# The first half's state sums by accumulating transposes, without pair additions, and a new order of the work

## The chip, the cores and the metric

The kernel runs on one core of a Trainium2 chip, in one launch. The metric is device time in microseconds from the first to the last instruction of the execution; the change is judged by the median of several executions. Engines are named as the profile names them: PE (TensorE), DVE (VectorE), ACT (ScalarE), POOL (GpSimd) and SP (SyncE, which only issues DMAs here).

## What is computed

Eight batches of 512 tokens with 128 features go through two layers, each of the form `x = x + s(xn) * silu(f(xn))` with `xn = layernorm(x)`. The first has attention and a mixture of 8 experts (top 2) side by side. The second has a Mamba block and 8 experts of which each token takes the best one:

```python
def _selective_scan(u, delta, A, Bm, Cm, D):
    def step(s, inp):
        d_t, B_t, C_t, u_t = inp
        s = s * exp(d_t[..., None] * A) + d_t[..., None] * B_t[:, None, :] * u_t[..., None]
        return (s, einsum('bds,bs->bd', s, C_t))
    ...
    return ys.swapaxes(0, 1) + u * D

scores = feats @ centroids.T
expert = argmax(scores, axis=1)
alpha = sigmoid(sum(feats * centroids[expert], axis=-1, keepdims=True))
```

The Mamba block has 256 inner channels (`d`, two halves of 128) and 16 states per channel; its input goes through an RMS norm first, `h = xn * rsqrt(mean(xn * xn) + eps)`. Each expert norms its input again.

## The kernel before

**Layout.** A tile is 128 partitions by 512. For the scan the partitions are inner channels and the columns are the 512 tokens of a batch, so half `h` (0 or 1) of the channels and state `n` (0 to 15) make scan step `s = 2n + h`, 32 steps per batch. For each step ACT computes the decay `dA` (step `d`), PE spreads row `n` of B over the partitions (`b`, into `b_row`), DVE multiplies it with `du` and runs the scan (L1328, L1341), POOL multiplies the state with row `n` of C (`p`, L1518). The products are summed over `n`: those of half 0 on PE into the PSUM bank `yacc`, by a matmul with the identity (`a`, L919), after a first product with `diagD` that adds `u * D` (L912); those of half 1 on POOL into `y1` (`e`, L1525), in the last batch on PE too (L927). The states live in few slots of `st` (three for half 0, two for half 1), so a scan waits until its slot's last user has been summed.

**Pair additions.** With `PAIRED = (4, 8, 12)`, DVE adds the products of states `n - 1` and `n` of half 0 (`q`, `add_pair`, L1347) and PE sums the result once, so 13 sums stand for 16 states.

**After the sums.** Step `y` (`c_step`, L1353 to L1360) gates both halves on DVE and writes them into `du`, reading `yacc` and reusing it for half 1; `op` projects them back (L936), and POOL or DVE adds the residual.

**Second experts.** ACT norms the tokens (`xm`) to `xn1_tok`, and scales them by `rstd2` to `ht_tok`, which shares memory with `rl`. PE transposes both (`hT`, L791; `x1T`, L787), ACT copies both out of PSUM. `sc` multiplies x1T with the centroids, DVE takes the maximum `am` and the choice (`first_max`), `rk` finds each token's place, and `put` scatters the rows of `xn1_tok` by an indirect DMA of POOL. The experts' work is group `F` (`w` loads of weights, `xs`, `h`, `y`), and `get` gathers their rows, `ft` and `silu` finish them.

**Order.** Nothing is planned while it runs. The table `ROWS` gives each step of each group a place in units of a batch (group A: attention and first experts, two batches ahead; H: norm to delta, one ahead; S: the scan; F: second experts; C: output of the batch before), a lag for ACT, DVE and POOL in 32nds of a batch, and a PSUM bank out of four. `OWN` gives the first two batches' A and H their own places, `P` rows prepare weights. `program(engine)` sorts all steps by place and lag; each engine works its own list strictly in that order and waits on semaphores where data come from another. `READY`, `EMPTY` and `BEFORE` count what each semaphore must have reached. So a step that waits holds all that stands behind it on its engine.

Of the kernel before, what the change touches and what calls it, by code (L numbers as in the profile page):

```python
# [28 lines left out]
E = 8  # L29
# [13 lines left out]
PAIRED = (4, 8, 12)  # L43
# [10 lines left out]
def adds_of_first(n):  # L54

    m, k = n % NS, n // NS
    return k * (NS - len(PAIRED)) + m + 1 - sum(1 for p in PAIRED if p <= m)


def group_tiles(k):  # L60
# [1544 lines left out]
```

## Time and profile before

| | |
|---|---|
| time, median of 3 runs | 950.92 us (949.97 to 953.21) |
| span of the profiled execution | 950.8 us, 15737 instructions |
| first scan starts | 133.4 us |
| scans of batch 7 start | 867.3 us |
| last DVE instruction starts | 947.5 us |
| mean granted PE clock | 0.951 |

```profile
DVE  3352678999889998999989998899899999998994
PEclk9997999999899989999999999999899998886998
L1341 DVE TENSOR_TENSOR_SCAN st<-dA,b_row 128x512 f32<-128x512 f32 x123 | 148.8, 1210 | 8.0 <-ACT dA L975 7.8
L1347 DVE TENSOR_TENSOR st<-st 128x512 f32<-128x512 f32 x24 | 28.2, 1175 | 0.9
L919 PE MATMUL yacc<-st,w_ident 128*128 128x512 f32 x208 | 115.7, 641 | 21.9 <-POOL st L1518 16.5 <-DVE st L1347 5.3
```

The first two lines cut the span into 40 equal slices and give the share in which DVE was busy, and the clock that PE was granted, in tenths. The others are groups of instructions of one form: how many, their busy time in us and the mean of one in ns, then how long the engine had been idle before them and which instruction ended that. An fp32 matmul of 512 columns leaves two records. PE is pipelined: a record is longer than the distance to the next.

### The profile page before, as it was taken

What the parts mean: (1) busy time and instruction counts of PE and PEld (TensorE: products, weight loads), DVE (VectorE), ACT (ScalarE), POOL (GpSimd) and SP (SyncE); (2) the same over time, 40 slices, a digit from 0 to 9 for tenths busy, and PEclk for the clock granted to TensorE, in tenths of its full rate; (3) what the DMA queues carried; (4) which work ended last, traced back from release to release, by engine and by line L of the source; (5) the groups of instructions that cost most, each with busy time, mean ns of one, the idle gap of its engine ahead of it and who ended that gap; (6) DMA issues with size and microseconds to landing.
All of it is one profiled execution on the core that took longest, in us unless ns stands there. A gap on an engine that the chain in (4) does not pass through costs nothing.

```text
span 950.8 us, 15737 instructions
## 1 busy us (share of the span) xinstructions
PE 831.6 (87%) x4576; PEld 575.2 (61%) x4576; DVE 798.4 (84%) x1503; ACT 629.8 (66%) x1379; POOL 604.9 (64%) x556
## 2 busy tenths in 40 slices
PE   4989999998899879998799869998899876866885
PEld 2767666764677547765576547765676644543552
DVE  3352678999889998999989998899899999998994
ACT  2534667777687856776687866776686865684561
POOL 0000125769585884769585885769585888788664
PEclk9997999999899989999999999999899998886998
DMA  7200122232332333232331333232331333343441
GB/s 261 101 1 1 47 73 85 75 114 78 119 98 77 110 108 82 77 109 80 118 103 68 103 118 84 81 103 86 108 108 62 106 113 107 105 110 103 149 128 38
DMA packets 79430, 90.29 MB, mean 95 GB/s; under 512 B 8450, under 2 KB 49906, under 8 KB 78834
## 3 DMA queue, kind: packets, MB, share of 16 engines
q1 hardware_dynamic: 77298, 85.07, 29.4%
q0 software_dynamic: 2048, 4.20, 1.5%
q8 instruction: 40, 0.66, 0.3%
q14 instruction: 44, 0.36, 0.1%
HBM read 52.96 MB, written 13.04 MB: 69 GB/s over the span
## 4 chain that ended last, share of the span: by engine, by line
PE 39%; DVE 38%; issue 11%; POOL 6%; ACT 5%; SPq 1%; DVEq 0%; DMA 0%; POOLq 0%; ACTq 0%
DVE st L1341 13%; PE work L849 7%; PE work L855 6%; DVE acc L1225 4%; DVE b_row L1328 3%; PE work L890 3%; PE work L880 3%; PE work L778 3%; DVE cv L1254 3%; DVE dbu L1328 3%; POOL st L1518 2%; PE yacc L919 2%; DVE st L1347 2%; ACT prob L975 1%; PE work L769 1%
## 5 line engine op out<-in xcount | busy, mean ns | idle before, releaser
L1518 POOL TENSOR_TENSOR st<-st,Cs 128x512 f32<-128x512 f32 x249 | 320.0, 1297 | 158.0 <-DVE st L1341 152.8
L975 ACT ACTIVATE dA<-delta,Aneg 128x512 f32<-128x512 f32 x256 | 177.7, 718 | 12.9 <-DVE st L1341 12.8
L1341 DVE TENSOR_TENSOR_SCAN st<-dA,b_row 128x512 f32<-128x512 f32 x123 | 148.8, 1210 | 8.0 <-ACT dA L975 7.8
L1341 DVE TENSOR_TENSOR_SCAN st<-dA,dbu 128x512 f32<-128x512 f32 x128 | 154.6, 1208 | 0.0
L1525 POOL TENSOR_TENSOR y<-y,st 128x512 f32<-128x512 f32 x105 | 138.1, 1315 | 3.8
L849 PE MATMUL work<-xnT,w_w1a 128*128 128x512 f32 x256 | 132.7, 612 | 8.5 <-DVE delta L1309 7.0
L855 PEld LDWEIGHTS work<-w_w2a,hid 128*128 128x128 f32 x1024 | 125.1, 196 | 23.4 <-issue 8.7
L919 PE MATMUL yacc<-st,w_ident 128*128 128x512 f32 x208 | 115.7, 641 | 21.9 <-POOL st L1518 16.5
L975 ACT ACTIVATE hsT<-work,hs 128x128 f32<-128x128 f32 x352 | 100.2, 370 | 46.5 <-PE work L880 45.9
L855 PE MATMUL work<-w_w2a,hid 128*128 128x128 f32 x1024 | 128.8, 280 | 0.7 <-ACT hid L975 0.6
L880 PEld LDWEIGHTS work<-xsT,hs 128*128 128x128 f32 x704 | 98.6, 207 | 25.1 <-issue 5.9
L975 ACT ACTIVATE hid<-work,w_b1a 128x512 f32<-128x512 f32 x128 | 86.2, 683 | 37.6 <-PE work L849 33.3
L880 PE MATMUL work<-xsT,hs 128*128 128x128 f32 x704 | 103.2, 294 | 2.6 <-ACT ys L975 1.4
L1225 DVE SCALAR_TENSOR_TENSOR acc<-work,gates,acc 128x128 f32<-128x128 f32 x256 | 71.3, 340 | 35.2 <-PE work L855 32.8
L890 PE MATMUL work<-w_w2f,hsT 128*128 x704 | 99.2, 284 | 0.0
L1328 DVE TENSOR_TENSOR dbu<-b_row,du 128x512 f32<-128x512 f32 x123 | 85.1, 692 | 13.2 <-PE b_row L903 5.9
L890 PEld LDWEIGHTS work<-w_w2f,hsT 128*128 128x128 f32 x704 | 86.0, 192 | 5.7 <-issue 3.0
L1328 DVE TENSOR_TENSOR b_row<-b_row,du 128x512 f32<-128x512 f32 x123 | 84.0, 683 | 2.7
L849 PEld LDWEIGHTS work<-xnT,w_w1a 128*128 128x128 f32 x256 | 43.4, 192 | 42.3 <-issue 17.1
L919 PEld LDWEIGHTS yacc<-st,w_ident 128*128 128x128 f32 x208 | 37.0, 202 | 52.7 <-POOL st L1518 25.4
L1488 POOL DMA_INDIRECT xs_dram<-xn_tok,pos x32 | 32.2, 1006 | 57.6 <-DVE pos L1303 51.2
L903 PE MATMUL b_row<-bc,sel_b 96*128 96x512 bf16 x123 | 48.5, 394 | 21.9 <-DVE st L1341 21.9
(191 smaller groups left out, 1290.9 us busy)
## 6 DMA issues: line engine op xcount, KB each, us to landing
Cs<-c_dram SPq DMA_DIRECT2D x128, 256.0 KB, 3.6
hs<-w_w1f SPq DMA_DIRECT2D x88, 258.0 KB, 2.3
xs_in<-xs_dram SPq DMA_DIRECT2D x16, 256.0 KB, 3.4
ys_dram<-ys SPq DMA_DIRECT2D x16, 256.0 KB, 2.9
w_w1f<-in_w1f_dram SPq DMA_DIRECT2D x1, 2064.0 KB, 8.0
x_in<-in_x_dram SPq DMA_DIRECT2D x8, 256.0 KB, 5.6
w_w2f<-in_w2f_dram SPq DMA_DIRECT2D x1, 2048.0 KB, 12.4
kept_dram<-x_tok SPq DMA_DIRECT2D x8, 256.0 KB, 4.0
```

The source lines that it names most:

```text
L849: last = mm(w[:], W["w1a"][:, i * 128:(i + 1) * 128], xnT[:], start=True, stop=True)
L855: last = mm(w[:, t * 128:(t + 1) * 128], hid[:, c % 4, t * 128:(t + 1) * 128], W["w2a"][:, c * 128:(c + 1) * 128], start=(c == PER * i), s ...
L880: last = mm(w[:, c * 128:(c + 1) * 128], w1s[:, i % 2, c * 128:(c + 1) * 128], xsT[:, i // 4 % 2, i % 4 * 128:(i % 4 + 1) * 128], start=Tr ...
L890: last = mm(r, hsT[:, i % 2, c * 128:(c + 1) * 128], W["w2f"][:, bass.ds(e * H1 + c * 128, 128)], start=False, stop=(c == HC - 1))
L903: mm(rows_bank(n, b)[:], row_of(n), bc3[:, par], start=True, stop=True).then_inc(sig["B_in"], 1)
L919: mm(yacc[:], ident[:], state(s), start=False, stop=(n == NS - 1)).then_inc(sig["y_sum0"], 1)
L975: return nc.scalar.activation(out, in_, func, **k)
L1225: last = V.scalar_tensor_tensor(acc[:, t], w[:, t * 128:(t + 1) * 128], gates[:, t, i:i + 1], acc[:, t], ALU.mult, ALU.add)
L1328: V.tensor_tensor((dbu0, rows_bank(n, b))[h][:], rows_bank(n, b)[:], du[:, par, h], ALU.mult).then_inc(sig["dBu"], 1)
L1341: V.tensor_tensor_scan(state(s), dA[:, s % DECAYS], (dbu0, rows_bank(n, b))[h][:], 0.0, ALU.mult, ALU.add).then_inc(sig["scan"], 1)
L1518: G.tensor_tensor(state(s), state(s), Cs[:, b.of(NS, n) % C_BUFS], ALU.mult).then_inc(sig["P"], 1)
L1525: G.tensor_tensor(y1[:], y1[:], state(s), ALU.add).then_inc(sig["y_sum1"], 1)
```

## The change

- The steps `q` and `PAIRED` are gone: every product of half 0 is summed by itself. The wait of a scan for its slot is now always for the sum.
- In batches 0 to 6 a sum of half 0 is four transposes of 128x128 with the state as stationary operand and the identity as moving one, accumulated into `yacc`, which then holds the sum with tokens on the partitions. After the last one ACT copies `yacc` into `delta[:, par, 0]` (new step `yt`), and PE forms `u * D` in a bank of `work` and adds four transposes of the copy to it (new step `yb`). DVE's `y` reads that bank. `yacc` is free once `yt` has read it.
- In batch 7 the sums stay identity matmuls, now 16, and `y` reads `yacc`.
- `x1T`, its transposes and its copy are gone. `sc` multiplies hT, which is scaled by `rstd2`, and DVE multiplies the maximum with `rms` (POOL: `q2 * rstd2`), the inverse of that scale.
- `ht_tok` has its own memory; `put` scatters its rows in place of those of `xn1_tok`, so `xm` waits for the `put` of the batch before. ACT's `dl` of half 1 waits for `sc`, since `rl` shares memory with hT.
- All places, lags of moved steps, own places and banks are new. On DVE, `y` of a batch now stands behind scans 0, 1 and 2 of the next batch and two sums of first experts (m6, m7), where it stood behind scan 0. On POOL, `ft` moved behind the first product of the next batch, and the four `get` stand among the last products of a batch.

```diff
-PAIRED = (4, 8, 12)
...
-    ("H", "x1T", 0, 0.46354, -1, 7, -3, 1),
-    ("S", "q", 4, 0.32753, 3, 1, 6, None),
-    ("S", "q", 8, 0.61830, 4, 0, 2, None),
-    ("S", "q", 12, 0.85132, -1, 0, 2, None),
...
+    ("C", "yt", 0, 0.15021, -5, 0, 0, None),
+    ("C", "yb", 0, 0.04512, 0, 0, 0, 0),
...
             def add_state(n, b):
 
                 s = NH * n
+                last = b.is_(NB - 1)
                 if n == 0:
                     if b.is_(0):
                         pe.wait_ge(prep_dve, 3)
-                    since(pe, sig["yo"], b.of(1))
-                    mm(yacc[:], diagD[:], u[:, b.n % 2, 0], start=True, stop=False)
-                if n + 1 in PAIRED:
+                    since(pe, sig["yt"], b.of(1))
+                    if last:
+                        mm(yacc[:], diagD[:], u[:, b.n % 2, 0], start=True, stop=False)
+                pe.wait_ge(sig["P"], b.of(STEPS, s + 1))
+                if last:
+                    mm(yacc[:], ident[:], state(s), start=False, stop=(n == NS - 1)).then_inc(sig["y_sum0"], 1)
                     return
-                if n in PAIRED:
-                    pe.wait_ge(sig["pair"], b.of(len(PAIRED), PAIRED.index(n) + 1))
-                else:
-                    pe.wait_ge(sig["P"], b.of(STEPS, s + 1))
-                mm(yacc[:], ident[:], state(s), start=False, stop=(n == NS - 1)).then_inc(sig["y_sum0"], 1)
+                for t in range(NT):
+                    add = mm(yacc[:, t * 128:(t + 1) * 128], state(s)[:, t * 128:(t + 1) * 128], ident[:], is_transpose=True,
+                             start=(n == 0 and t == 0), stop=(n == NS - 1), skip_group_check=True)
+                add.then_inc(sig["y_sum0"], 1)
+
+            def turn_back(g, step, b):
+
+                par = b.n % 2
+                w = bank(g, step, b)
+                bank_free(pe, g, step, b)
+                pe.wait_ge(sig["yt"], b.of(1, 1))
+                mm(w[:], diagD[:], u[:, par, 0], start=True, stop=False, skip_group_check=True)
+                for t in range(NT):
+                    part = slice(t * 128, (t + 1) * 128)
+                    last = mm(w[:, part], delta[:, par, 0, part], ident[:], is_transpose=True, start=False, stop=True,
+                              skip_group_check=True)
+                last.then_inc(ready[g], 1)
...
+                    since(act, sig["put"], b.of(16 * NT))
...
+                elif g == "C" and name == "yt" and not b.is_(NB - 1):
+                    act.wait_ge(sig["y_sum0"], b.of(NS, NS))
+                    go(delta[:, b.n % 2, 0], yacc[:], ACT.Copy).then_inc(sig["yt"], 1)
...
+                    dve.wait_ge(sig["rms"], b.of(1, 1))
+                    V.tensor_tensor(am[:], am[:], rms[:], ALU.mult)
...
-            def add_pair(n, b):
-
-                dve.wait_ge(sig["P"], b.of(STEPS, NH * n + 1))
-                V.tensor_tensor(state(NH * n), state(NH * n), state(NH * (n - 1)), ALU.add).then_inc(sig["pair"], 1)
...
+                    if not last:
+                        dve.wait_ge(sig["yo"], b.of(1, 1))
+                        dve.sem_inc(free_of("C", ("yb", 0), b), 1)
```

## Rows read from the trace of the kernel before

**Rows 1.** The page, busy time and chain that ended last.
```profile
PE 831.6 (87%) x4576; PEld 575.2 (61%) x4576; DVE 798.4 (84%) x1503; ACT 629.8 (66%) x1379; POOL 604.9 (64%) x556
...
PE 39%; DVE 38%; issue 11%; POOL 6%; ACT 5%; SPq 1%; DVEq 0%; DMA 0%; POOLq 0%; ACTq 0%
```

**Rows 2.** Windows: stretch, busy us (x) of each engine, PEclk, DMA share, GB/s.
```profile
455.00:561.00 106.00, 95.43 (x560) 66.95 (x560) 98.00 (x185) 78.25 (x172) 78.22 (x72) 1.00 0.31 97
...
775.00:867.00 92.00, 64.32 (x299) 41.63 (x299) 86.10 (x122) 56.07 (x126) 73.54 (x67) 0.82 0.37 106
867.00:951.00 84.00, 64.84 (x309) 40.46 (x307) 66.08 (x79) 39.65 (x99) 54.24 (x43) 0.93 0.37 112
```

**Rows 3.** Timeline of DVE, start and length in us.
```profile
242.55 0.69 DVE L1353 TENSOR_TENSOR du<-yacc,zg 128x512 f32<-128x512 f32 x1
...
778.45 0.69 DVE L1353 TENSOR_TENSOR du<-yacc,zg 128x512 f32<-128x512 f32 x1
```

**Rows 4.** Waits of DVE from 247 to 785 us: total, times, longest.
```profile
DVE gm L1196 <- PE work L748: 6.2, 5, 2.2
...
DVE nmax L1192 <- PE work L763: 1.8, 5, 0.4
```

**Rows 5.** Timeline of DVE, first and third pair addition of a steady batch.
```profile
492.51 0.92 DVE L1347 TENSOR_TENSOR st<-st 128x512 f32<-128x512 f32 x1
493.35 1.11 DVE L1225 SCALAR_TENSOR_TENSOR acc<-work,gates,acc 128x128 f32<-128x128 f32 x4
...
543.58 1.42 DVE L1347 TENSOR_TENSOR st<-st 128x512 f32<-128x512 f32 x1
544.91 0.69 DVE L1307 SCALAR_TENSOR_TENSOR work<-work,ez 128x512 f32<-128x512 f32 x1
```

**Rows 6.** Timeline of DVE, pair additions of batches 6 and 7.
```profile
851.34 4.00 DVE L1347 TENSOR_TENSOR st<-st 128x512 f32<-128x512 f32 x1
855.27 0.69 DVE L1307 SCALAR_TENSOR_TENSOR work<-work,ez 128x512 f32<-128x512 f32 x1
...
926.79 0.67 DVE L1347 TENSOR_TENSOR st<-st 128x512 f32<-128x512 f32 x1
927.37 0.69 DVE L1328 TENSOR_TENSOR work<-work,du 128x512 f32<-128x512 f32 x1
```

**Rows 7.** Timeline of DVE, a small operation behind a drain.
```profile
468.84 0.19 DVE L1204 SCALAR_TENSOR_TENSOR eq<-gt,w_first 128x32 f32<-128x32 f32 x1 [0.21 <-DVE ot L1368]
```

**Rows 8.** Timeline of PE, a sum and four transposes in a full queue.
```profile
462.41 0.60 PE L744 MATMUL work<-w_ident,qkv 128*128 128x128 f32 x4
462.85 0.22 PE L888 MATMUL work<-b2p,sel_b 96*128 96x128 bf16 x1
...
501.82 1.02 PE L919 MATMUL yacc<-st,w_ident 128*128 128x512 f32 x2
502.68 0.38 PE L903 MATMUL b_row<-bc,sel_b 96*128 96x512 bf16 x1
```

**Rows 9.** Groups of instructions by form: count, busy us, mean ns, idle before.
```profile
L787 PE MATMUL work<-w_ident,xn_tok 128*128 128x128 f32 x32 | 4.8, 272 | 0.0
...
L975 ACT ACTIVATE xn1T<-work 128x512 f32<-128x512 f32 x8 | 4.7, 589 | 0.0
...
L1505 POOL DMA_INDIRECT fe<-ys_dram,pos x32 | 31.1, 972 | 7.5 <-issue 6.6
```

**Rows 10.** Timeline of DVE between batches 6 and 7.
```profile
870.47 0.69 DVE L1353 TENSOR_TENSOR du<-yacc,zg 128x512 f32<-128x512 f32 x1 [1.95 <-PE yacc L919]
...
873.30 0.76 DVE L1357 SCALAR_TENSOR_TENSOR yacc<-u,w_dskip,y 128x512 f32<-128x512 f32 x1 [2.14 <-POOL y L1525]
```

**Rows 11.** Timelines of PE and POOL at the end of a batch.
```profile
558.60 1.12 PE L919 MATMUL yacc<-st,w_ident 128*128 128x512 f32 x2 [0.88 <-POOL st L1518]
...
554.82 4.95 POOL L1518 TENSOR_TENSOR st<-st,Cs 128x512 f32<-128x512 f32 x4
```

More of the change, by code:

```diff
@@ L403, with turned_not @@
 TAKEN_AT = {("A", ("o", 0)): ("o", NT - 1)}
+def turned_not(step, b):
+    return step == ("C", ("yb", 0)) and b == NB - 1
 READY = {}
@@ L408 @@
 for _g, _s, _b in ORDER:
-    if (_g, _s) in BANK:
+    if (_g, _s) in BANK and not turned_not((_g, _s), _b):
         READY[_g, _s, _b] = 1 + sum(1 for g, s, b in READY if g == _g)
     _job = _g, TAKEN_AT.get((_g, _s), _s), _b
-    if _job[:2] in BANK and _job not in EMPTY:
+    if _job[:2] in BANK and _job not in EMPTY and not turned_not(_job[:2], _b):
         _k = bank_of(*_job)
@@ L495, in build @@
         hx = sb("hx", [128, NH, T])
-        ht_tok, hT = hx[:, 0].rearrange("p (i d) -> p i d", i=NT), hx[:, 1]
+        hT = hx[:, 1]
         rl = hx
@@ L515, in build @@
         rstd2 = sb("rstd2", [128, NT])
+        rms = sb("rms", [128, NT])
         shift, shift1 = sb("shift", [128, NT]), sb("shift1", [128, NT])
@@ L518, in build @@
         xn1_tok = sb("xn1_tok", [128, 2, NT, D])
-        xn1T = sb("xn1T", [128, T])
+        ht_tok = sb("ht_tok", [128, NT, D])
         u = sb("u", [128, 2, NH, T])
@@ L783, in a_step @@
                         last = nc.tensor.transpose(w[0:E, t * 128:(t + 1) * 128], gates[:, t], ident[:])
-                elif name == "x1T":
-                    pe.wait_ge(sig["xn1"], b.of(1, 1))
-                    for t in range(NT):
-                        last = nc.tensor.transpose(w[:, t * 128:(t + 1) * 128], xn1_tok[:, par, t], ident[:])
                 elif name == "hT":
@@ L800, in a_step @@
                 elif name == "sc":
-                    emptied(pe, g, ("x1T", 0), b)
+                    emptied(pe, g, ("hT", 0), b)
                     if b.is_(0):
@@ L953, in do @@
                     project(g, step, b)
+                elif g == "C" and name == "yb" and not b.is_(NB - 1):
+                    turn_back(g, step, b)
                 elif g == "P" and name == "pe":
@@ L1024, in a_step @@
                     go(tiles(bank(g, ("m", E - 1), b)[:]), acc[:], ACT.Tanh).then_inc(sig["siluA_e"], 1)
-                elif name == "x1T":
-                    filled(act, g, step, b)
-                    go(xn1T[:], w[:], ACT.Copy).then_inc(fr, 1)
                 elif name == "hT":
@@ L1351, in c_step @@
                 if step[0] == "y":
-                    dve.wait_ge(sig["y_sum0"], adds_of_first(b.of(NS, NS - 1)))
-                    V.tensor_tensor(du[:, par, 0], yacc[:], zg[:, par, 0], ALU.mult).then_inc(sig["y0"], 1)
+                    last = b.is_(NB - 1)
+                    if last:
+                        dve.wait_ge(sig["y_sum0"], b.of(NS, NS))
+                        r = yacc
+                    else:
+                        filled(dve, "C", ("yb", 0), b)
+                        r = bank("C", ("yb", 0), b)
+                    V.tensor_tensor(du[:, par, 0], r[:], zg[:, par, 0], ALU.mult).then_inc(sig["y0"], 1)
                     dve.wait_ge(sig["y_sum1"], b.of(NS, NS))
                     dve.wait_ge(sig["y0"], b.of(1, 1))
-                    second = work[SPARE] if b.is_(NB - 1) else y1
-                    V.scalar_tensor_tensor(yacc[:], u[:, par, 1], W["dskip"][:, 1:2], second[:], ALU.mult, ALU.add
+                    second = work[SPARE] if last else y1
+                    V.scalar_tensor_tensor(r[:], u[:, par, 1], W["dskip"][:, 1:2], second[:], ALU.mult, ALU.add
                                            ).then_inc(sig["y1"], 1)
                     dve.wait_ge(sig["y1"], b.of(1, 1))
-                    V.tensor_tensor(du[:, par, 1], yacc[:], zg[:, par, 1], ALU.mult).then_inc(sig["yo"], 1)
+                    V.tensor_tensor(du[:, par, 1], r[:], zg[:, par, 1], ALU.mult).then_inc(sig["yo"], 1)
+                    if not last:
+                        dve.wait_ge(sig["yo"], b.of(1, 1))
+                        dve.sem_inc(free_of("C", ("yb", 0), b), 1)
                 elif step[0] == "op":
@@ L1386, in do @@
                     scan(i, b)
-                elif g == "S" and name == "q":
-                    add_pair(i, b)
                 elif g == "C":
@@ L1476, in a_step @@
                         G.tensor_tensor(rstd2[:], q2[:], neghalf[:], ALU.pow).then_inc(sig["rstd1"], 1)
+                        pool.wait_ge(sig["rstd1"], b.of(1, 1))
+                        since(pool, sig["hot"], b.of(1))
+                        G.tensor_tensor(rms[:], q2[:], rstd2[:], ALU.mult).then_inc(sig["rms"], 1)
                 elif name == "du":
@@ L1489, in a_step @@
                                          bass.IndirectOffsetOnAxis(pos[:, par, i:i + 1], 0),
-                                         xn1_tok[:, par, i], None).then_inc(sig["put"], 16)
+                                         ht_tok[:, i], None).then_inc(sig["put"], 16)
             def f_step(step, b):
```

19 lines of the change are left out of this document (8 added, 11 removed), and 548 rows, old and new, of tables (OWN, OWN_BANKS, ROWS, sig).

## The prediction

> **What bounds the kernel now.** I read the busy times first [rows 1]: TensorE 87%, VectorE 84%, ScalarE and GpSimd two thirds, and the chain that ended last is split between TensorE and VectorE. An average of that kind names no bound, so the windows by period came next [rows 2]. In steady state a batch takes 107.2 us: the first product of a batch's output (L1353) starts at 242.6 us and, five batches on, at 778.5 us [rows 3]. In such a stretch of 106 us VectorE's records cover 98 us and TensorE's 95.4 us. In the last two stretches, where no later batch's attention is left, TensorE falls to 64 us of 92 and VectorE stays near 94% of the first of them.
>
> What VectorE's remaining 8 us are decides. Part of them are drains of about 0.2 us between dependent small operations. What it waits for others in five steady periods is 26.2 us in seven rows of the waits, 6.2 down to 1.8 us [rows 4], 5.2 us per period; five of the seven, 3.7 us per period, name TensorE as the releaser. So VectorE runs without a hole apart from 5 us: whatever is taken off its queue comes off the period, if TensorE follows. TensorE has about 10 us of holes per period, so it isn't the first bound but a close second.
>
> **Pair additions (VectorE).** The three `q` steps per batch go. Their price is the distance from their start to the next instruction's, since records overlap: 0.84, 0.90 and 1.33 us in one steady period (the first and the last of the three in [rows 5]), 3.07 us. For batches 0 to 5: 6 x 3.07 = 18.4 us. In batch 6 the third held the engine 3.93 us, in batch 7 each took 0.58 us [rows 6]: 0.84 + 0.90 + 3.93 = 5.7 us and 1.8 us. The spread has a reason: the add reads two SBUF tensors, and the dear ones stand beside a train of GpSimd products. The GPSIMD Engine Reference of the Trainium skill (Specifications) says that GpSimd shares its SBUF interfaces with VectorE where the latter has two SBUF inputs; the trace agrees, 0.58 us where GpSimd pauses and 3.93 us beside its train. What stands next in VectorE's queue there mostly reads PSUM, so I count the whole of it as gone. Sum: 25.9 us.
>
> **Additions to VectorE.** One 128x4 multiplication by `rms` per batch and, in seven batches, a wait for its own last product before the bank is given back. Neither is in the trace; the nearest row is a small operation of 0.19 us behind a drain of 0.21 us [rows 7]. Bounds 0.1 and 0.4 us for each, taken 0.2: 15 x 0.2 = 3.0 us lost.
>
> **The sums (TensorE).** A sum by identity matmul takes 0.86 us start to start in a full queue; four 128x128 fp32 transposes take 0.44 us [rows 8]. Before, 13 sums: 11.2 us per batch; after, 16 sums in seven batches: 7.0 us. The turn back adds four transposes (0.44), the x1T transposes go (0.44), the diagD product only moves. Saved: 4.1 us per period. The other bound: the state is now the stationary operand, so its load can't start ahead of the product as the identity's could, and four transposes alone last 0.60 us by the length of their record [rows 8]. Then 17 x 0.16 = 2.7 us are given back and 1.5 us remain. I take the full queue's value, since most sums stand behind other matmuls. None of it is on the path by itself; it buys cover for the waits of [rows 4]. In batch 7 the sums stay identity matmuls, 16 in place of 13, 2.6 us on an engine with 20 us of holes: nothing.
>
> **ScalarE** loses the copy of x1T and gains the copy of `yt`, 0.59 us each [rows 9]. GpSimd gains one 128x4 product per batch. `put` now sends rows of the single ht_tok, so `xm` of the next batch waits for it; in the new queues some 20 scans lie between them. Nothing for each. The last batch's `dl` wait for `sc` is met long before.
>
> **The end of a batch.** The output's path grows: last sum, ScalarE copy, TensorE turn back, then VectorE's `y`. Sorting the rows by place and lag gives the new queues: VectorE reaches `y` after scan 2 of the next batch, the products m6 and m7, and `silu`; before it stood behind scan 0 and `silu`. So the path has some 6 us more cover (two scans with their inputs 3.6, m6 and m7 2.4) for 1.9 us more work (copy 0.59, turn back 0.86 + 0.44). Where this matters is between batches 6 and 7: today VectorE stands 1.95 us for the sums and 2.14 us for the GpSimd half [rows 10]. Two more scans stand ahead of it now, and GpSimd's `ft` goes behind; of 4.1 us I take 3, bounds 0 and 4.1.
>
> **The new places.** They can't be priced by rows. The score maximum `gl`, the dearest of the waits [rows 4], stands three operations later, and TensorE has 4 us more room; of 5.2 us per period I take 1 in six periods, 6 us; bounds from 1 us worse to 3.7 us better (all that TensorE causes). In the last batch GpSimd issues its gathers between the last products instead of before them: four issues of about 1.25 us with their gaps [rows 9] now partly behind the last scan, about 1 us lost. The stages before the first scan (133 us) lose 0.44 us of TensorE work and are laid anew: nothing, within 3 us.
>
> **Sum.** 25.9 - 3.0 + 3 + 6 - 1 = 30.9 us. The profiled execution spans 950.8 us, 0.1 us under the median of 950.92 (949.97 to 953.21): 920.
>
> **Rivals.** (a) A wait takes the freed time. TensorE saves only 1.5 us, the waits stay (minus 6), the 3 us between batches stay, and the new order costs 1 us per period (7): 936. For it: TensorE is busy 95 of 106 us, and the holes of a new order can't be read from this trace. Against: it needs both at once. 18%.
> (b) The order does better: 3.7 of 5.2 us go in six periods, 16 more: 904. 11%.
> (c) TensorE's clock. In batch 6, where its queue thins, the granted clock is 0.82 against 1.00 [rows 2]. The new sums thin it too. TensorE's 91.3 us per period at 0.82 are 111.3 us, so it would bind, 4.1 us over today's period: +25 for six periods, less the 10.5 us of batches 6 and 7: 965, slower. It decides from a clock of 91.3 / 103 = 0.89 down. TensorE's page of the Trainium skill (TensorE: Matmul & The Clock Gate, Part 4) says that PE-mode transposes don't count as busy for the clock in the way matmuls do; by that rule this rival is the likely one where sums fill a thin stretch. This trace doesn't show it: the transposes it has (16 of prob per batch among them) lie in a period granted 1.00 [rows 2]. Against: transposes would be 7.4 us of 91. 3%.
> (d) A transpose with a fresh stationary state takes its own 272 ns [rows 9], not 110: 17 x 4 x 0.16 = 11 us more, TensorE 102 us plus its 10 us of holes: a period of 113, +34 less 10.5: 974, slower. 2%.
> (e) ScalarE blocks at `yt`: its queue holds the tanh and the next decays behind a wait for the last sum. Today four products run as a train, and the last sum starts 1.2 us before that train ends [rows 11]. In the new queues, counted from the end of delta, GpSimd has two du products, P29, a gather and P30 ahead of the last sum (6 us), sum and copy end at 7; VectorE has scans 29, 30, 31, 0, m6, m7, 1 and 2 ahead of the `silu` that needs the tanh (13 us). So 6 us of cover; each us beyond costs 7 us in all, and it is slower from 11 us on; at 12 us 962. 2%.
> (f) The additions weren't what held the scans, and all of their time comes back as waits for the same sums: 950.8 less the 3 us between batches, 948, no change. 2%. The main case: 62%.
>
> **Chances.** Faster by over 0.3% (2.9 us; about what a measurement of this kernel can tell from no change): 0.92, within: 0.02, slower: 0.06. Range 907 to 937: it takes in (a) and leaves half of (b) and all of (c) to (f) out, some 15 in 100, the rest being for bounds not met.
>
> **What would show it.** No L1347 rows; steady periods of 103 to 104 us; VectorE's covered time per period near 95 us with 4 us of waits; TensorE's near 91 us, the four-transpose sum 0.44 us start to start, the clock at 0.95 or more; no wait above 1 us at L1353 before the last batch. A TensorE-bound period (its holes under 5 us while VectorE's grow), or VectorE waiting for the bank of `yb`, would make the prediction wrong.

## The result and the profile after

The changed kernel takes 945.51 us, median of 9 runs (943.44 to 947.6), the one before 953.7 us in the same session (949.97 to 957.45): ratio 0.9913, 95% interval 0.9894 to 0.9932. Of the 30.9 us that were forecast, 8 came. The profiled execution spans 943.7 us. From its page, the busy times and the engines of the chain that ended last, which answer [rows 1]:

```profile
PE 815.7 (86%) x4844; PEld 607.9 (64%) x4844; DVE 799.8 (85%) x1487; ACT 630.5 (67%) x1378; POOL 597.8 (63%) x564
...
PE 42%; DVE 36%; issue 12%; ACT 5%; POOL 3%; DMA 1%; SPq 1%; DVEq 0%; POOLq 0%; ACTq 0%
```

TensorE's records cover 16 us less, VectorE's cover as much as before, although 24 additions of 128x512 are gone. Two facts stand in these lines already: something on VectorE grew, and TensorE, with less to do, leads the chain more than before.

**Where the time went.** The first scan of each batch cuts the execution (starts of the first of its 32 scans in VectorE's timeline; batch 7 ends with its last scan):

| stretch, us | before | after | forecast |
|---|---|---|---|
| start to first scan | 133.4 | 123.4 | same within 3 |
| batches 0 to 5 | 641.5 | 648.5 | 22 less |
| batch 6 | 92.4 | 90.3 | |
| batch 7 to its last scan | 65.4 | 63.8 | with batch 6 some 10 less |

So the loss is mainly in the steady batches, 7 us slower instead of 22 faster, and the stages before them gave 10 us that the forecast had put at nothing. Without these 10 us the changed kernel would not have been faster at all. The windows of batches 0 to 5, before and after (stretch, busy us of each engine, PEclk, DMA share, GB/s):

```profile
133.00:775.00 642.00, 587.13 (x3366) 412.46 (x3364) 586.42 (x1100) 469.82 (x1036) 463.09 (x421) 0.97 0.32 95
```
```profile
123.00:772.00 649.00, 577.54 (x3576) 437.42 (x3574) 588.64 (x1077) 470.36 (x1031) 453.84 (x422) 0.94 0.31 94
```

The granted clock fell from 0.97 to 0.94. Summed over windows of 1 us, 34 us of this part were at 1.2 GHz before and 71.5 us after; all numbers "at 1.2 GHz" below are such sums.

**VectorE's ledger, batches 0 to 5** (from each start to the next, waits apart): pair additions 18.1 to 0; waits for `b_row` 4.8 to 18.6; four small operations with two SBUF inputs 19 us more in sum; all idle times above 0.15 us together 38.6 to 43.4. The waits of VectorE after (total, times, longest), where [rows 4] had `gm` and `nmax`:

```profile
DVE dbu L1346 <- PE b_row L898: 18.6, 18, 2.3
DVE acc L1241 <- PE work L850: 8.4, 17, 1.1
```

**The first new cost: TensorE's clock.** TensorE's timeline at the end of batch 3 (start, length; in brackets the idle time before and its releaser), and the same stretch in windows:

```profile
541.61 0.39 PE L898 MATMUL b_row<-bc,sel_b 96*128 96x512 bf16 x1 [1.56 <-DVE st L1357]
541.84 1.02 PE L844 MATMUL work<-xnT,w_w1a 128*128 128x512 f32 x2
545.37 1.34 PE L844 MATMUL work<-xnT,w_w1a 128*128 128x512 f32 x2 [2.50 <-DVE delta L1327]
...
550.96 2.91 PE L850 MATMUL work<-w_w2a,hid 128*128 128x128 f32 x16
553.71 0.38 PE L898 MATMUL b_row<-bc,sel_b 96*128 96x512 bf16 x1
```
```profile
541.00:545.30 4.30, 1.25 (x3) 0.40 (x3) 4.23 (x7) 3.58 (x6) 3.27 (x4) 1.00 0.65 212
...
546.00:549.00 3.00, 2.22 (x9) 1.51 (x8) 2.97 (x4) 1.28 (x3) 2.77 (x6) 0.52 0.07 22
549.00:553.00 4.00, 4.00 (x15) 2.97 (x14) 2.92 (x4) 2.65 (x5) 3.84 (x4) 0.50 0.40 133
```

TensorE works 1.25 of 4.3 us, waiting for the last broadcast and for `delta`; then the clock stands at 0.5 for 7 us, of which it works 6.2. The 16 products of 128x128 take 2.91 us instead of 2.0, the next batch's first row of b goes out at 553.71, and VectorE stands for it:

```profile
554.18 0.70 DVE L1346 TENSOR_TENSOR dbu<-b_row,du 128x512 f32<-128x512 f32 x1 [2.26 <-PE b_row L898]
```

The sums themselves cost what the prediction had: in a full queue at the full clock the four transposes take 0.44 us from start to start (median of 69), a matmul with the identity 0.86 (51 of them before).

```profile
517.12 0.60 PE L915 MATMUL yacc<-w_ident,st 128*128 128x128 f32 x4
517.56 1.02 PE L844 MATMUL work<-xnT,w_w1a 128*128 128x512 f32 x2
```

**The second: small operations beside GpSimd.** VectorE and GpSimd of the changed kernel at the second gate:

```profile
513.38 0.19 DVE L1186 TENSOR_TENSOR eq<-work,am 128x32 f32<-128x32 f32 x1
513.60 1.21 DVE L1187 TENSOR_TENSOR eq<-eq,w_first 128x32 f32<-128x32 f32 x1
514.85 0.19 DVE L1188 TENSOR_REDUCE gr<-eq 128x4 f32<-128x32 f32 x1
515.07 0.97 DVE L1189 TENSOR_TENSOR ohr<-eq,gr 128x32 f32<-128x32 f32 x1
```
```profile
513.50 1.26 POOL L1539 TENSOR_TENSOR st<-st,Cs 128x512 f32<-128x512 f32 x1
514.73 1.26 POOL L1546 TENSOR_TENSOR y<-y,st 128x512 f32<-128x512 f32 x1
```

L1187 begins 0.1 us behind a GpSimd product and ends with it (514.81 and 514.76), L1189 behind the next and ends with that (516.04 and 515.99). The reduction between them has one input, L1186 reads one of its two from PSUM: neither is touched. (The 256 scans aren't either, 1.21 us beside GpSimd or not: one of their inputs, `b_row` or `dbu`, lies in PSUM.) Before, L1187's counterpart took 0.19 us at this place. The pattern repeats in every batch, and again at the first gate (1.18 and 0.97 us).

### The profile page after: what moved, and what is told of

Its sections match the earlier page's. It is cut to its first block, busy times and chain, and to the rows that moved or that the text cites. A ratio compares the mean times of both kernels' runs of the same rounds, so it can differ in the third digit from the quotient of the medians.

```text
span 943.7 us, 16309 instructions
## 1 busy us (share of the span) xinstructions
PE 815.7 (86%) x4844; PEld 607.9 (64%) x4844; DVE 799.8 (85%) x1487; ACT 630.5 (67%) x1378; POOL 597.8 (63%) x564
## 4 chain that ended last, share of the span: by engine, by line
PE 42%; DVE 36%; issue 12%; ACT 5%; POOL 3%; DMA 1%; SPq 1%; DVEq 0%; POOLq 0%; ACTq 0%
DVE st L1357 10%; PE work L850 9%; PE work L844 9%; DVE b_row L1346 4%; PE work L777 3%; DVE cv L1270 3%; DVE acc L1241 3%; PE work L875 3%; DVE dbu L1346 2%; PE work L885 2%; PE work L761 2%; PE yacc L915 2%; PE work L768 2%; POOL st L1539 1%; PE yacc L977 1%
## 5 line engine op out<-in xcount | busy, mean ns | idle before, releaser
L844 PE MATMUL work<-xnT,w_w1a 128*128 128x512 f32 x256 | 137.2, 626 | 16.8 <-DVE delta L1327 15.0
L850 PEld LDWEIGHTS work<-w_w2a,hid 128*128 128x128 f32 x1024 | 131.3, 205 | 18.2 <-issue 15.0
L850 PE MATMUL work<-w_w2a,hid 128*128 128x128 f32 x1024 | 134.2, 288 | 3.5 <-ACT hid L988 3.5
L1546 POOL TENSOR_TENSOR y<-y,st 128x512 f32<-128x512 f32 x105 | 133.5, 1271 | 5.2
L885 PE MATMUL work<-w_w2f,hsT 128*128 x704 | 102.5, 290 | 0.0
L885 PEld LDWEIGHTS work<-w_w2f,hsT 128*128 128x128 f32 x704 | 88.3, 197 | 3.2 <-issue 1.2
L915 PE MATMUL yacc<-w_ident,st 128*128 128x128 f32 x448 | 72.6, 291 | 3.6 <-POOL st L1539 3.6
L915 PEld LDWEIGHTS yacc<-w_ident,st 128*128 128x128 f32 x448 | 59.2, 155 | 20.4 <-issue 15.2
L1509 POOL DMA_INDIRECT xs_dram<-ht_tok,pos x32 | 32.2, 1006 | 61.8 <-DVE pos L1321 55.5
```

Of the source, the lines that this page charges most:

```text
L844: last = mm(w[:], W["w1a"][:, i * 128:(i + 1) * 128], xnT[:], start=True, stop=True)
L850: last = mm(w[:, t * 128:(t + 1) * 128], hid[:, c % 4, t * 128:(t + 1) * 128], W["w2a"][:, c * 128:(c + 1) * 128], start=(c == PER * i), s ...
L885: last = mm(r, hsT[:, i % 2, c * 128:(c + 1) * 128], W["w2f"][:, bass.ds(e * H1 + c * 128, 128)], start=False, stop=(c == HC - 1))
L915: add = mm(yacc[:, t * 128:(t + 1) * 128], state(s)[:, t * 128:(t + 1) * 128], ident[:], is_transpose=True, start=(n == 0 and t == 0), sto ...
L1546: G.tensor_tensor(y1[:], y1[:], state(s), ALU.add).then_inc(sig["y_sum1"], 1)
```

## The experiments

Two theories stood at first. *Places*: the mechanics give what was forecast, and the new places lose it. *Mechanics*: what VectorE is spared comes back wherever the places are. All times below are medians; ratios are to the kernel before, run beside them, with their 95% intervals.

**The mechanics on the old places, the pair additions alone, identity sums on the new places, b's first row earlier.**

> All mechanics of the change (no pair additions, sums by accumulating transposes, the copies yt and yb, scores without the rows of their own) on the places of before; only the additions of m 3 and m 7 are put a little earlier, and yt and yb stand just ahead of their readers. Places theory (the mechanics are worth what was forecast, and the new places lost it in the periods, through waits for b_row, 13.8 us more in batches 0 to 5, and through some 20 us of small VectorE operations that stand beside GpSimd's; their prologue gave 10 us back): the periods fall from 107.2 to 103 or 104 us, the time before the first scan stays at 133 us, and the whole is about 925 us (918 to 933). Mechanics theory (what VectorE is spared comes back wherever the places are, since the additions and drains only exchange one contention for another and TensorE sets the rest): the periods stay at 107 to 109 us and the whole is 945 to 957 us.

```diff
-PAIRED = (4, 8, 12)
+("C", "yt", 0, 0.00800, 0, 0, 0, None)
+("C", "yb", 0, 0.03150, 0, 0, 0, 0)
...
```

999.7 us, 1.0468 (1.0404 to 1.0532): batches 0 to 5 took 675 us. Neither theory had that. TensorE waits for x^T because `yb` keeps its bank (waits of PE there; L1366 is the give back of that bank):

```profile
PE work L729 <- DVEq L1366: 14.0, 5, 2.8
```

> The kernel before with the pair additions taken away and nothing else: TensorE sums all 16 states of the first half by matmuls with the identity, 3 more per batch (about 2.6 us of it per batch at 0.86 us each). If the freed VectorE time (3.07 us per period, 25.9 us in all by the profile of before) is really gone, the whole falls by 15 to 25 us, to 929 to 939 us. If the pair additions' time was contention that the next VectorE operations inherit (they took 0.6 us each when GpSimd rested), no more than 3 x 0.6 us per period and some 3 us at batches 6 and 7 go: 12 us at most, less what TensorE has to do more: 941 to 953 us.

```diff
-PAIRED = (4, 8, 12)
+PAIRED = ()
...
-    ("S", "q", 4, 0.32753, 3, 1, 6, None),
```

The edit also moves the sums of states 3 and 7, which the pairs had made needless, to earlier places, 0.352 and 0.567. 956.5 us, 1.0029 (1.0006 to 1.0052). In the old order the step that I had counted at 25.9 us is worth nothing when TensorE has to sum the three states more with the identity. The additions' time went (18.1 us), and these waits of VectorE came, of which the kernel before has neither:

```profile
DVE st L1324 <- PE yacc L902: 12.5, 12, 1.1
DVE work L1290 <- ACT cv L958: 6.6, 6, 1.2
```

A scan needs the buffer of an older state, which a pair gave back by VectorE's own addition and which TensorE's sum now gives back later. How much of the loss is this wait and how much TensorE's three sums more per batch wasn't separated.

> The changed kernel with its new places, but the first half's states summed by 16 matmuls with the identity in every batch as it does in the last one: no accumulating transposes, no copies yt and yb turned back. It costs TensorE about 0.42 us more per sum, some 6 us per period net of the turn back. Places theory: TensorE waits 12 us in a period of 109 us, so most of it is hidden; the whole is 945 to 960 us. If TensorE sets the period of the changed kernel, all of it shows: 945 + 6 x 6 to 7 = 981 us or more.

```diff
-                last = b.is_(NB - 1)
+                last = True
...
-                    since(pe, sig["yt"], b.of(1))
+                    since(pe, sig["yo"], b.of(1))
```

960.8 us, 1.0074 (1.0048 to 1.0099). At the upper edge of what the places theory expected: the transposes are worth 15 us.

> The changed kernel with one place moved: the broadcast of b's first row for the next batch goes ahead of the feed-forward products h14 and m6 on TensorE. Places theory: VectorE's wait for it at the first gated product (2.26 us per period) goes, the whole falls by 6 to 12 us, to 934 to 940 us. Rival (the wait only stands where the period's slack collects, since TensorE is behind anyway): another wait of VectorE takes its place, the whole stays within 3 us of 945.

```diff
-    ("S", "b", 0, -0.08101, 4, 1, 1, None),
+    ("S", "b", 0, -0.10300, 4, 1, 1, None),
```

943.6 us, 0.9895 (0.9855 to 0.9934). The rival's result. The wait for `b_row` fell from 18.6 to 6.2 us, the wait for the products of m rose by 9.3: so the lateness seems to be TensorE's and not that of one step. In all four runs the time at 1.2 GHz in batches 0 to 5 differed: 78, 31, 55 and 65 us. That made the clock the next suspect.

**The idle places filled.** A third theory: TensorE, spared work, idles long enough at two places for the clock to fall, and what it does next is late.

> The changed kernel with six more matmuls per period on TensorE, of zeros by 512 columns, added into yacc in the middle of its sum: two ahead of the last broadcast of b, four ahead of h 13, where TensorE stands idle for 1.6 and 2.5 us and where the records then show 6.8 us at 1.2 GHz in nearly every period (546 to 553 us among them); they add zero, so the result is the same. In the changed kernel 71.5 us between 135 and 775 us are at 1.2 GHz, in the one before 34.2. Clock theory (TensorE sets much of the period, and the time that it was spared returns as stretches at 1.2 GHz that follow its idle time): the 34 us of low clock at this place go, TensorE is some 2.5 us earlier in each period, and the whole falls by 5 to 12 us to 933 to 940. Rival (the clock is low only where TensorE is not late): the low stretches go, or move, and the whole stays within 3 us of 945. Third (the clock falls because of the transposes and not of idle time): the low stretches stay and the six matmuls cost up to 5 us.

```diff
+FILLS = {('S', ('b', 15)): (2, False), ('A', ('h', 13)): (4, False)}
...
+                    mm(yacc[:], zeros[:, 0:1].broadcast_to([128, 128]), W["w1a"][:, 0:512], start=first, stop=False,
+                       skip_group_check=True)
```

929.6 us, 0.9746 (0.9716 to 0.9776): 16 us less by work that computes nothing ("the filling" below), more than I expected. 10 us at 1.2 GHz remain in batches 0 to 5. The stretch that answers the one shown above, and the windows of batches 0 to 5:

```profile
532.75 0.39 PE L901 MATMUL b_row<-bc,sel_b 96*128 96x512 bf16 x1
532.98 1.02 PE L847 MATMUL work<-xnT,w_w1a 128*128 128x512 f32 x2
533.84 3.59 PE L986 MATMUL yacc<-w_w1a,zeros 128*128 128x512 f32 x8
537.27 1.02 PE L847 MATMUL work<-xnT,w_w1a 128*128 128x512 f32 x2
...
540.86 1.95 PE L853 MATMUL work<-w_w2a,hid 128*128 128x128 f32 x16
542.65 0.38 PE L901 MATMUL b_row<-bc,sel_b 96*128 96x512 bf16 x1
```
```profile
124.00:756.00 632.00, 580.72 (x3647) 428.82 (x3647) 587.46 (x1076) 469.68 (x1030) 454.40 (x422) 0.99 0.32 96
```

The four zero products last 3.6 us, more than the hole that they fill, and still the broadcast comes 9.9 us after the last one of its batch (542.65 less 532.75) instead of 12.1 (553.71 less 541.61). VectorE's wait for `b_row` is 12 us shorter, out of 16 us by which its idle time fell; the time of its operations is the same within 1 us.

> As the run with six matmuls of zeros, at the same two places and for the same time, but each of the six is four transposes of 128 x 128 zeros instead of one matmul over 512 columns. If the chip counts transposes as no work, as the Trainium skill has it (TensorE: Matmul & The Clock Gate, Part 4), the stretches at 1.2 GHz stay where they are in the changed kernel and the time is 945 us or up to 5 us more. If they count like matmuls, clock and time are those of the run with matmuls, within 2 us.

```diff
-                    mm(yacc[:], zeros[:, 0:1].broadcast_to([128, 128]), W["w1a"][:, 0:512], ...)
+                    for t in range(NT):
+                        mm(yacc[:, t * 128:(t + 1) * 128], zeros[:, 0:1].broadcast_to([128, 128]), ident[:],
+                           is_transpose=True, ...)
```

928.9 us, 0.9747 (0.9717 to 0.9777), 7 us at 1.2 GHz. At these two places transposes of fp32 zeros hold the clock as well as matmuls of zeros do. The rule of the Trainium skill (TensorE: Matmul & The Clock Gate, Part 4), by which they don't count, isn't borne out here.

> The run with b's first row ahead of h14 and m6, and with the six matmuls of zeros, and three more of them at the start of the period (one ahead of the second transposes of the feed-forward input, two ahead of x^T), where TensorE waits 0.8 and 1.0 us and where 3.4 to 6.8 us at 1.2 GHz follow in most periods. Clock theory: low clock between 135 and 775 us falls from 65 us to under 25, the whole to 928 to 936 us. Rival (waits decide, not the clock): within 3 us of 943.6.

The edit joins the earlier place of b 0 and the filling, with `('F', ('xs', 1)): (1, True)` and `('A', ('xT', 0)): (2, True)` added. 935.2 us, 0.9808 (0.9778 to 0.9838). The clock did as expected (10 us low), the time did not: 5.6 us worse than the run with six. The likely reason is that a filling costs where TensorE's queue is full behind it; the earlier place of b 0 and the three matmuls more weren't tried apart at this clock.

> The changed kernel with its accumulating transposes and its places, and the three pair additions per batch back on VectorE where they stood before; TensorE turns and sums 13 states instead of 16. If VectorE's queue sets the changed kernel's period, it is longer by the pair additions, 2 to 3 us per batch: 958 to 968 us. If TensorE sets it, the 1.3 us of transposes per batch that go are worth as much as the additions cost, and the whole stays at 940 to 950 us. The kernel before without its pair additions came out at +0.3%, which speaks for the second.

```diff
+                if n + 1 in PAIRED:
+                    return
...
+                V.tensor_tensor(state(NH * n), state(NH * n), state(NH * (n - 1)), ALU.add).then_inc(sig["pair"], 1)
```

The additions stand on almost their old places (the first at 0.345 instead of 0.328, all without their lags). 976.2 us, 1.0241 (1.0212 to 1.027), beyond both expectations, with 109 us at 1.2 GHz. So in the new order the additions' going is worth much, in the old one nothing; part of that may be that nothing else was laid anew for them.

**Is it the filling or the change?**

> The kernel before, unchanged but for nine matmuls of zeros per period at TensorE's idle places: two into yacc ahead of the last broadcast of b (idle 1.5 us), two into yacc ahead of h 13 (1.4 us), five into the bank of the next product ahead of the second transposes of the feed-forward input (2.5 us). In the kernel before 34.2 us between 133 and 775 us are at 1.2 GHz. If the clock costs it as much per us as it cost the changed kernel (71.5 to 10.2 us at 1.2 GHz there were 16 us of time), 24 us less at 1.2 GHz bring 6 us: 944 to 950 us; the change is then worth some 17 us at a like clock, against 930 us of the changed kernel with its matmuls of zeros. If TensorE sets nothing in the kernel before, it stays at 953 us or is up to 3 us longer. If it falls to 935 us or less, most of the 16 us belong to the matmuls of zeros and not to the change.

```diff
+FILLS = {('S', ('b', 15)): 2, ('A', ('h', 13)): 2}
+FILLS_OF = {('F', ('xs', 1)): (('h', 0), 5)}
```

955.4 us, 1.0035 (1.0004 to 1.0066), at 3 us of 1.2 GHz. The kernel before does not gain from this filling:

```profile
135.00:777.00 642.00, 617.22 (x3475) 424.97 (x3474) 586.31 (x1099) 469.74 (x1035) 462.91 (x421) 1.00 0.32 95
```

VectorE's waits in batches 0 to 5 stayed as they were. TensorE is now busy for 617 of 642 us, so a gain from the clock and the cost of nine matmuls per batch may cancel; the run doesn't tell these apart. With matmuls of zeros in both kernels the change is worth 955.4 less 929.6, 26 us: 11 of them before the first scan (135.5 and 124.5 us) and only 9.5 in batches 0 to 5 (641.6 and 632.1).

> The changed kernel with the six matmuls of zeros, and one place more moved: the small operations of the second gate (L1187 and L1189 of the changed kernel among them) on VectorE one scan earlier, where the kernel before has them. In the changed kernel they stand beside GpSimd's products and two of them take 1.2 and 1.0 us instead of 0.19: about 1.8 us per period. Contention theory: they find GpSimd at rest as before, the two fall to 0.2 us, VectorE's queue is 1.8 us shorter per period and, since it is VectorE that is full now, the whole falls by 5 to 10 us to 920 to 925 us. Rival (GpSimd runs beside them there as well, or the products' scores are not there yet and VectorE waits as long): within 3 us of 929.6.

```diff
-    ("H", "sc", 0, 0.53826, 9, 1, -3, 1),
+    ("H", "sc", 0, 0.53826, 9, 0, -3, 1),
```

948.3 us, 0.9965 (0.9939 to 0.9991). Wrong for both: the small operations were stretched at the earlier place as well (1.2 us less in six batches), and the clock fell elsewhere, 34 us at 1.2 GHz. Here a move on VectorE undid the filling on TensorE.

> All mechanics of the change on the places of before, as in the run that took 1000 us, but x^T goes to work bank 2 instead of bank 0, which yb holds until VectorE has read it; in that run x^T waited 2.8 us per batch for it. Bank theory: that wait goes, and with it idle time of TensorE and the low clock that follows it; periods of 112.5 us come down to 107 to 109, the whole to 955 to 970 us. Rival (the bank only passes a wait on that some other step has): still 990 to 1000 us.

> The run before this one (mechanics of the change, places of before, x^T in bank 2) with the six matmuls of zeros per period ahead of the last broadcast of b and of h 13. If the clock is what the old places lost, it comes to 935 to 945 us, near the changed kernel with the same matmuls (929.6 us), and the new places are worth mainly the 10 us of their prologue. If the new places are needed for the order of waits itself, it stays 20 us or more above 929.6 us.

```diff
-    ("A", "xT", 0, 0.07492, -1, 3, 4, 0),
+    ("A", "xT", 0, 0.07492, -1, 3, 4, 2),
```

The second run has the lines of `FILLS` as well. 984.0 and 984.2 us, 1.0340 (1.0297 to 1.0383) and 1.0344 (1.0303 to 1.0386). The bank explains 16 of the 47 us that the first run lost. With the other bank 68 us were at 1.2 GHz, with the filling too 71: at these two places the filling doesn't hold the clock of this order. The mechanics need an order of their own; what else the old one lacks for them wasn't followed further.

**The parts at a held clock.**

> The changed kernel with the first half's states summed by matmuls with the identity instead of transposes, and the six matmuls of zeros per period. Without the matmuls of zeros it took 960.8 us with 55 us at 1.2 GHz in the periods. If its loss against the changed kernel (15 us) was the clock's and not TensorE's work, it comes to 935 us or less. If TensorE's extra 6 us of work per period count as soon as the clock is held, since then there is little idle time to hide them, it stays 25 to 35 us above 929.6 us: 950 to 965 us.

954.2 us, 1.0033 (1.0008 to 1.0059), 20 us at 1.2 GHz. TensorE's extra work counts: the transposes are worth 24.6 us in this order, 18.7 of them in batches 0 to 5, 3.1 per batch. That is half of the work that they spare against 16 sums by identity, 16 x 0.42 less 0.44 for the turn back, 6.3 us.

> The changed kernel with the three pair additions per batch back on VectorE, and the six matmuls of zeros per period. Without the matmuls of zeros it took 976 us with 109 us at 1.2 GHz. If VectorE's queue sets the period when the clock is held, the additions cost what they take, 12 to 18 us in the periods and 3 to 8 us behind them: 943 to 955 us. If it stays above 965 us, the additions hurt through something else than their own time, a wait for the pair that TensorE and the scans stand behind.

978.8 us in the profiled execution and 984.7 in another (clocks 0.945 and 0.933); four more took 995 to 997 us at a clock of 0.90. Above 965 by any: the additions hurt through more than their 17.6 us. Batches 0 to 5 take 39.6 us more than with the filling alone. And though the time at 1.2 GHz fell from 109 to 44 us, it is no faster than without the filling (976.2), so the clock doesn't explain this loss. Waits of VectorE that the run with the filling alone has not, or hardly:

```profile
DVE st L1370 <- PE yacc L919: 10.1, 6, 1.7
...
DVE bc L1299 <- ACT bc L999: 7.9, 6, 2.6
```

**The contention.**

> The changed kernel with the six matmuls of zeros, and one GpSimd product per batch (that of scan 18) held back until VectorE's small operations of the second gate are done. Contention theory: the product of scan 18 ran beside L1187 (1.2 us instead of 0.19); held back, L1187 takes 0.2 us, and L1189 0.2 us unless the addition to y stands beside it; VectorE's queue is 1 to 1.8 us shorter per period, the product starts about 1 us later, and the whole is 929.6 us less 0 to 8 us, if TensorE's clock stays as it is. Rival (the small operation waits for something of its own): it takes 1.2 us as before.

```diff
                 pool.wait_ge(sig["scan"], b.of(STEPS, s + 1))
+                if s == 18 and not b.is_(NB - 1):
+                    pool.wait_ge(sig["hot"], b.of(1, 2))
```

925.7 us, 0.9711 (0.9669 to 0.9753): 4 us less, in the expected range. L1187 and L1189 lost 10.8 us in batches 0 to 5; a part came back as waits, with 27 us at 1.2 GHz instead of 10.

> The changed kernel with the six matmuls of zeros per period, the product of scan 18 held back as in the run that took 925.7 us, and also GpSimd's addition for the output held back until VectorE's gates are done (L1220 and L1222 of the changed kernel, 1.2 and 1.0 us beside it). Contention theory: these two fall to 0.2 us, 1.8 us less per period on VectorE; GpSimd's next sums start 3 us later. If they have slack the whole is 918 to 925 us; if the scans wait for them, it is 925 to 935 us.

```diff
                     pool.wait_ge(sig["xr"], b.of(16, 16))
+                    if b.n + 3 < NB:
+                        pool.wait_ge(sig["gates"], b.of(1, 4))
```

912.4 us, 0.9605 (0.9571 to 0.9638), better than expected, and the fastest version: 38 us under the kernel before. First VectorE at the second gate in this run, then GpSimd, released by `ohb`:

```profile
599.95 0.19 DVE L1197 TENSOR_TENSOR eq<-eq,w_first 128x32 f32<-128x32 f32 x1
600.18 0.19 DVE L1198 TENSOR_REDUCE gr<-eq 128x4 f32<-128x32 f32 x1
600.40 0.19 DVE L1199 TENSOR_TENSOR ohr<-eq,gr 128x32 f32<-128x32 f32 x1
```
```profile
601.10 1.27 POOL L1551 TENSOR_TENSOR st<-st,Cs 128x512 f32<-128x512 f32 x1 [1.21 <-DVE ohb L1308]
```

The groups of the four operations by form (busy us, mean ns), in the changed kernel and in this run:

```profile
L1187 DVE TENSOR_TENSOR eq<-eq,w_first 128x32 f32<-128x32 f32 x16 | 10.2, 637 | 0.5
...
L1189 DVE TENSOR_TENSOR ohr<-eq,gr 128x32 f32<-128x32 f32 x8 | 7.0, 874 | 0.3
...
L1220 DVE SCALAR_TENSOR_TENSOR eq<-gt,w_first 128x32 f32<-128x32 f32 x8 | 6.4, 805 | 1.4 <-DVE ot L1388 1.1 <-ACT gp L988 0.3
...
L1222 DVE TENSOR_TENSOR oh<-eq,gr 128x32 f32<-128x32 f32 x8 | 6.3, 786 | 0.3
```
```profile
L1197 DVE TENSOR_TENSOR eq<-eq,w_first 128x32 f32<-128x32 f32 x16 | 3.1, 191 | 0.5
...
L1232 DVE TENSOR_TENSOR oh<-eq,gr 128x32 f32<-128x32 f32 x8 | 2.4, 300 | 0.3
...
L1199 DVE TENSOR_TENSOR ohr<-eq,gr 128x32 f32<-128x32 f32 x8 | 1.5, 191 | 0.3
...
L1230 DVE SCALAR_TENSOR_TENSOR eq<-gt,w_first 128x32 f32<-128x32 f32 x8 | 1.5, 187 | 1.4 <-DVE ot L1398 1.1 <-ACT gp L998 0.3
```

29.9 us became 8.5. The windows of batches 0 to 5 show the periods at 617.3 / 6 = 102.9 us, with VectorE covered for 95 us of each. That is 24 us less than in the kernel before (641.5), where the forecast had 22:

```profile
123.00:740.00 617.00, 577.86 (x3646) 428.22 (x3645) 570.54 (x1076) 469.44 (x1030) 453.29 (x422) 0.99 0.33 98
```

**The end and the start.**

> The changed kernel with the six matmuls of zeros per period and 33 more in the last two batches, ahead of waits of 1.7 to 5.0 us that TensorE has there (among them 8 ahead of the first transposes of the feed-forward input of the last batch, 6 ahead of its last sum, 4 ahead of its last projection). There 25 to 30 us between 780 us and the end are at 1.2 GHz; the last projection takes 3.6 us at it where it took 2.0 at 2.4 GHz. If the clock matters there as in the periods: 3 to 6 us less than 929.6. If the end is a chain of VectorE and GpSimd that TensorE is no part of but for the last projection: 0 to 2 us less.

The edit adds counts at six steps of batches 6 and 7 and four products ahead of the last projection. 933.8 us, 0.9793 (0.9751 to 0.9835): a miss, 4 us slower than without. Batch 6 took 96.7 us instead of 90.7, although less time was at 1.2 GHz. So more time at the full clock did not help there; presumably the 33 matmuls stood in the way.

> The changed kernel with the own places of batch 0's attention and first feed-forward part, and of the weight preparations, put back to those of the kernel before; batch 0's state part and batch 1's own places stay new. In the changed kernel the first scan stands at 123.4 us, before at 133.4. If the order of batch 0's first part brought the 10 us, the first scan is at 130 to 135 us and the whole at 952 to 958 us; if batch 1's places did (its work fills TensorE's waits), it stays at 123 to 126 us and the whole at 945.

The edit puts back the `("A", 0)` tuple with its banks and the seven `P` rows. 959.1 us, 1.0104 (1.0064 to 1.0145), the first scan at 137.6 us: the order of the first batch and of the preparations brought the 10 us, and with the rest new the old one is 4 us worse than it was. Without it the change makes the kernel slower.

## Why the prediction failed, by its steps

The forecast was 920 us and the result is 945.5. The way was right by luck: all of the gain of 8 us came from the stages before the first scan, which the prediction had put at nothing, and with their old order the kernel takes 959.1 us. The steps that failed lie in batches 0 to 5, forecast 22 us less and measured 7 more. The filling (16 us in all) and holding GpSimd back (15 us there, 632.1 to 617.3) together took them from 648.5 to 617.3, 31 us.

- **"Whatever is taken off its queue comes off the period, if TensorE follows."** The condition was the weak point. TensorE followed in work (0.44 us per sum against 0.86, as in [rows 8]; the lower bound that I gave as 1.5 us comes to 1.4) but not in time: it idled longer at two places of each batch and then ran at 1.2 GHz. Filling them gave 16 us. Why the holes are there in this order and not in the old one stays open.
- **The pair additions, "so I count the whole of it as gone".** The 18.4 us of batches 0 to 5 measured 18.1 and went. But [rows 5] and [rows 6] had shown that they were dear for GpSimd beside them, and I looked only at what stands next in their own place. New places put the two gates beside GpSimd's products, and 128x32 operations of 0.19 us took 1.2: 19 us. Holding GpSimd back at both brought 17 us (929.6 to 912.4; 13 by the ratios, 0.9746 to 0.9605).
- **The new places, 6 us better, "bounds from 1 us worse to 3.7 us better" per period.** This failed most: six batches were to gain 6 us. The waits for `gl` and `nmax` did go down, by 7.6 us, and `dA` by 3.6; `b_row` cost 13.8 more, and the stretched operations belong here too. The bounds came from the waits of the old order alone; a new order can make waits that the old one has not.
- **Stages before the first scan, "nothing, within 3 us".** It was 10 us, from the new order of batch 0's first part and of the preparations, which wasn't worked out.
- **Batches 6 and 7**: 3.7 us less up to the last scan, forecast some 10. The pair additions went (8.2 us where I had 7.5), the two waits at the change of batch fell by 3.4 (forecast 3) and three others (`dA`, `am`, `cv`) by 2.3; against them stand 2.6 us of waits for `b_row`, 2.2 us of products of m that now fall behind batch 6's first scan, and some 5 us of small operations and other waits. The run with the filling there was slower with less time at 1.2 GHz, which speaks against the clock as the cause; more wasn't tried.
- **Rival (c), the clock, 3%.** This was one of the two mechanisms, at 0.94 and not 0.82, so it took gain but didn't make the whole slower. I gave it little because [rows 2] show a period at 1.00, a single one: over batches 0 to 5 the kernel before had 0.97. Its argument, that transposes don't count, isn't borne out; idle time was the reason, since filling it with either kind of product brought the clock back. Rival (a), a wait takes the freed time, was right in kind (13.8 us of waits for `b_row`) but not in its sizes: it had 936. Rival (d) didn't show (0.44 us per sum), nor did (e): ScalarE stood 9.7 us before six copies `yt`, 1.6 each, under its cover of 6. (f) didn't either, though the old order without the pair additions (956.5 us) behaves as it says.
- **The signs that I named**: periods of 103 to 104 us, VectorE's cover near 95 and a clock of 0.95 or more all failed (108.1, 98, 0.94), and so did TensorE's near 91 us (96.3, in part at 1.2 GHz). In the run at 912.4 us the first three are met (102.9, 95, 0.99). The four-transpose sum of 0.44 us and no wait above 1 us at the first product of the output held.

The forecast of 920 was thus a sum whose prices for the additions and the sums held. It lacked two couplings between engines that an order decides: what a product of GpSimd does to VectorE's operations, and what TensorE's idle time does to its clock.

## What to carry to other kernels

When work is taken off an engine with a clock of its own, ask where its idle time will gather, and look at the granted clock behind each such place before and after; filling it with products that add zero is a quick test. It brought 16 us at two places here, and nothing or a loss at others and in other orders. A VectorE operation with both inputs in SBUF costs at least what the GpSimd product beside it has left to run, however small it is (0.19 us became 1.21), so a change of order must be read on both queues. And one part of a change run alone on the old order (956.5 us) or taken out of the new one (976.2 us) can tell opposite tales: both are needed, and neither is a price of the part alone.

## What the hardware showed

- A VectorE operation of 128x32 with both inputs in SBUF takes 0.19 us alone and up to 1.21 us when it begins just behind a GpSimd product of 128x512, ending with it; with one input in PSUM it is not held (0.19 us). A pair addition of 128x512, 0.67 us with GpSimd at rest, took 4.00 us beside a train of GpSimd instructions in the kernel before [rows 6]. The Trainium skill (SBUF — State Buffer, SBUF: two separate sides) calls the shared pair an exclusive lock for the whole instruction; the traces agree.
- In the stretch shown TensorE fell to 1.2 GHz after working 1.25 us of 4.3, its longest single idle time being 2.50 us. Transposes of zeros in the same holes kept it at 2.4 GHz as matmuls of zeros did (7 and 10 us low in six batches).
- Matmuls of zeros that took the time at 1.2 GHz from 34 to 3 us brought the kernel before nothing (952 and 955 us); those that took it from 71.5 to 10 us brought the changed one 16 us.
